# Fourth stage: layer norm moments and roots one step ahead, and its normalising split in pairs between the two exps of two steps

## The reference

```
def _layernorm(x, axis=-1, eps=1e-05):
    m = jnp.mean(x, axis=axis, keepdims=True)
    v = jnp.var(x, axis=axis, keepdims=True)
    return (x - m) / jnp.sqrt(v + eps)
...
    qkv = jnp.einsum('bsd,ed->bse', x, Wqkv)
    ... 16 heads of 8 features
    logits = jnp.einsum('bihd,bjhd->bhij', q, k) * scale + pos_bias[None]
    attn = jax.nn.softmax(logits, axis=-1)
    out = jnp.einsum('bhij,bjhd->bihd', attn, v).reshape(B, S, D)
    return jnp.einsum('bsd,ed->bse', out, Wout)
...
x = x + _L1_attn_ref(_layernorm(x, axis=-1), L1_attn_Wqkv, L1_attn_Wout, L1_attn_Wpos, L1_attn_coeffs)
```

## Time and profile before

| | |
|---|---|
| median of 3 runs | 1625.31 us (1624.47 to 1625.8) |
| profiled execution | 1624.52 us, its span 1622.7 us |
| PE busy | 1510.8 us (93%) |
| DVE busy | 959.7 us (59%) |
| ACT busy | 832.2 us (51%) |
| POOL busy | 588.4 us (36%) |
| granted TensorE clock, mean | 0.977 |
| fourth stage | from the first bias at 824.7 us to the last output projection at 1070.4 us |

### The profile page before, as it was taken

How to read it: one execution, slowest core, us unless ns; L and a number is a source line. 1 busy time by engine, 2 the same in 40 slices (tenths; PEclk the granted TensorE clock), 3 DMA queues, 4 the chain that set the end, 5 groups by cost and what they waited for, 6 DMA issues and landing times.

```text
span 1622.7 us, 39378 instructions
## 1 busy us (share of the span) xinstructions
PE 1510.8 (93%) x15207; PEld 1153.5 (71%) x15207; DVE 959.7 (59%) x2605; ACT 832.2 (51%) x1574; POOL 588.4 (36%) x583
## 2 busy tenths in 40 slices
PE   6999999997999899999988888959999999998998
PEld 5777776665777777777656666647888888885765
DVE  3344443446778756565568878855556766766223
ACT  4554455445777533343456666635556555553431
POOL 4343445424222101111166666632323344434024
PEclk9999999998999999999999999979999999999999
DMA  5021230000000099100000000000000000000323
GB/s 151 16 60 40 61 106 7 12 1 8 8 10 10 2 379 384 65 0 0 1 1 2 2 2 2 2 13 1 6 6 6 12 11 9 7 9 25 97 77 87
DMA packets 76527, 68.85 MB, mean 42 GB/s; under 512 B 19533, under 2 KB 57034, under 8 KB 76234
## 3 DMA queue, kind: packets, MB, share of 16 engines
q1 hardware_dynamic: 74314, 62.36, 11.9%
q0 software_dynamic: 2048, 4.20, 0.8%
HBM read 24.58 MB, written 41.96 MB: 41 GB/s over the span
## 4 chain that ended last, share of the span: by engine, by line
PE 69%; issue 10%; DVE 9%; ACT 6%; POOL 4%; DMA 1%; SPq 1%; POOLq 0%; DVEq 0%; ACTq 0%
PE bank L1874 7%; PE bank L1866 7%; PE bank L2394 5%; PE bank L2362 5%; PE bank L1508 5%; PE bank L2356 4%; PE bank L1492 4%; PE bank L2373 4%; PE bank L2385 3%; PE bank L853 2%; PE bank L3019 2%; PE bank L873 2%; PE bank L826 2%; PE bank L3008 2%; PE bank L3010 2%
## 5 line engine op out<-in xcount | busy, mean ns | idle before, releaser
L1291 ACT COPY s_pT<-bank 77x512 f32<-77x512 f32 (+1 forms) x256 | 134.7, 585 | 91.1 <-PE bank L1492 90.8
L2184 POOL TENSOR_TENSOR s_p<-s_p,s_inverse 128x616 f32<-128x616 f32 x64 | 78.2, 1228 | 229.7 <-DVE s_inverse L2307 229.7
L1492 PE MATMUL bank<-ident,s_p 128*77 128x128 f32 (+1 forms) x1024 | 138.3, 281 | 21.1 <-ACT s_p L1284 20.6
L1726 ACT ACTIVATE s_hT<-bank,w_s_b 128x512 f32<-128x512 f32 x128 | 87.2, 687 | 126.2 <-PE bank L1866 125.1
L1492 PEld LDWEIGHTS bank<-ident,s_p 128*77 128x77 f32 (+1 forms) x1024 | 114.4, 146 | 49.8 <-ACT s_p L1284 31.1
L1874 PEld LDWEIGHTS bank<-w_s_w2T,s_hT 128*128 128x128 f32 x1024 | 122.3, 192 | 26.8 <-issue 15.3
L1195 POOL TENSOR_TENSOR s_p<-s_p,s_peak 128x1024 f32<-128x1024 f32 x64 | 120.0, 1896 | 37.9 <-DVE s_peak L1371 37.9
L1874 PE MATMUL bank<-w_s_w2T,s_hT 128*128 128x128 f32 x1024 | 124.4, 276 | 2.2 <-ACT s_hT L1726 2.2
L1866 PE MATMUL bank<-s_ln_xnT,w_s_w1T 128*128 128x512 f32 x256 | 121.6, 603 | 0.0
L1284 ACT ACTIVATE s_p<-s_p 128x616 f32<-128x616 f32 (+1 forms) x128 | 109.8, 892 | 20.6 <-POOL s_p L1195 16.4
L1827 DVE SCALAR_TENSOR_TENSOR s_total<-bank,s_combine,s_total 128x128 f32<-128x128 f32 x256 | 72.1, 344 | 74.6 <-PE bank L1874 73.2
(11 more groups left out here) (302 smaller groups left out, 3455.0 us busy)
## 6 DMA issues: line engine op xcount, KB each, us to landing
sorted_tokens<-s_zero SPq DMA_DIRECT2D x8, 4096.0 KB, 29.5
s_rows<-sorted_tokens SPq DMA_DIRECT2D x48, 64.0 KB, 1.9
routed_tokens<-s_routed SPq DMA_DIRECT2D x12, 256.0 KB, 2.4
x_all<-x SPq DMA_DIRECT2D x8, 256.0 KB, 3.2
w_s_gateup<-s_gateup SPq DMA_DIRECT2D x1, 2048.0 KB
out<-x_all SPq DMA_DIRECT2D x8, 256.0 KB, 2.7
w_s_k<-ctxT SPq DMA_DIRECT2D x8, 154.0 KB, 2.2
s_ctx<-ctxT SPq DMA_DIRECT2D x8, 154.0 KB, 2.5
```

Of the source, the lines that this page charges most:

```text
L1291: nc.scalar.copy(pT[0:keys, b % 2, 4 * q:4 * q + 4, :].rearrange("m h t -> m (h t)"), bank[0:keys, flip_bank("p", b, q), :]).then_inc(drai ...
L1492: last = nc.tensor.transpose(bank[0:keys, into, j * T:(j + 1) * T], p[:, b % 2, 4 * q + j, :], core.ident[:, :])
L1726: nc.scalar.activation(hT[:, e % 2, c, :], bank[:, HIDDEN + k % 4, :], ACT.Gelu, bias=w.s3_b1[:, k:k + 1]).then_inc(hT_ready, 1)
L2184: nc.gpsimd.tensor_tensor(part, part, inverse[:, b % 2, heads].unsqueeze(2).to_broadcast([P, HU, M]), ALU.mult).then_inc(share_ready, 1)
```

## The change

In the fourth stage alone (the second keeps its order), and for the groups from the second on:

- DVE takes the moments of the next group one step earlier, at the end of step 3 of the group before (`norm_steps` is 0, 3, 7, 11, 15, 19, 23 in place of 0, 4, 8, ...). The first entry stays at step 0, so for the group that is normalised in steps 1 and 2 nothing moves here.
- POOL's four root operations move with them: behind `lower` of the last batch of a group and ahead of `own_of` and `lower` of the next. A wait for `xn_ready` of the group before is added ahead of them, since `rstd` and `shift` have one buffer.
- ACT's four ACTIVATEs at the end of step 1 become two pairs, which stand between exp half 0 and exp half 1: batches 0 and 1 in step 1, batches 2 and 3 in step 2.

The PE program and all shapes and counts of instructions stay.

```diff
+    norm_steps = [G * g if cross or g == 0 else G * g - 1 for g in range(GROUPS - 1)]
...
         def rstd_of(g):
             pool.wait_ge(moments_ready, g + 1)
+            if g and not cross:
+                pool.wait_ge(xn_ready, G * g)
...
-            if g < GROUPS and b % G == 0:
-                rstd_of(g)
+            if b in norm_steps:
+                rstd_of(norm_steps.index(b) + 1)
...
-        def xn_of(g):
+        def xn_of(g, batches=range(G)):
...
-            for n in range(G):
+            for n in batches:
...
             if b >= 0:
                 exp_of(b, 0)
+            if not cross and step % G in (1, 2) and g < GROUPS:
+                xn_of(g, range(step % G * 2 - 2, step % G * 2))
...
-            if step % G == 1 and g < GROUPS:
+            if cross and step % G == 1 and g < GROUPS:
                 xn_of(g)
...
-            if step % G == 0 and g < GROUPS:
-                moments_of(g)
+            if step in norm_steps:
+                moments_of(norm_steps.index(step) + 1)
```

## The result

| | before | after |
|---|---|---|
| median | 1625.24 us (4 runs, 1624.47 to 1625.8) | 1602.14 us (4 runs, 1600.66 to 1602.82) |
| ratio | | 0.9857, 95% interval 0.984 to 0.9874 |
| profiled execution | 1624.52 us, span 1622.7 | 1602.82 us, span 1601.0 |
| granted clock, mean | 0.977 | 0.984 |
| fourth stage, first scores to last output projection | 823.47 to 1070.39: 246.9 us | 823.97 to 1047.07: 223.1 us |

The kernel is 23.1 us faster; 1601.5 was forecast. Two later measurements of the same kernel gave 1601.39 and 1602.24. In the profiled executions the stage alone is 23.8 us shorter, where the sum had 23.7.

A forecast was written before the change was run, and what follows sets the result against it. TensorE was busy 93% of the span; in the fourth stage its waits and a lowered clock bound the norm groups. Six groups at 3.95 us, 23.7, took 1624.52 to 1600.8, plus 0.8: 1601.5 us, range 1598.5 to 1605.

The forecast's parts named there:

- the sum: Fourth stage: 0.89 + 1.56 + 1.67 = 4.1 us a group, taken as 3.95 after the walk; six groups, 23.7 us.
- The moments: Step 1: DVE's bias and `add_to_x` come 1.26 us sooner, so PE's weighing starts 0.89 us sooner.
- the cover: End of step 3: DVE's 1.56 us wait for the scores takes in the moved moments' 1.26 us at no cost.
- The ACTIVATEs: Step 2: the first exp no longer stands behind four normalising ACTIVATEs on ACT; gain 1.56 us a group.
- The clock: Step 2's weighing: without the 1.77 us idle the clock stays up; 1.67 us a group regained, bounds 0 and 1.67.
- What is late next: Step 3: PE's exp hangs on POOL's lowering, behind DVE's bias of step 2; it costs 0.1 us.
- The walk: One group followed link by link through four engines: 26.7 us against 30.68, steps of 6.24, 6.72, 6.22 and 7.55.
- the prediction's 0.1 for them: POOL's moved roots cost between nothing and 1.73 us; 0.1 taken, with keys ready 0.7 us before the scores.
- The second group's norm: Stage's steps 1 and 2: held exp costs at most 1.0 us, at best gives 1.56; taken as 0.
- The signs: Profile after: about 26.7 us a group, no exp wait above 0.5 from the second group, PEclk 1.00 from the first.
- thin covers: Rival: idle times barely hold the moved work; the roots' 1.73 us coming through gives 13.3 us, 1612; chance 0.04.
- fall all the same: Rival: the clock still falls on short idles, leaving 2.3 us a group, 13.7 in all: 1611.6; chance 0.07.

The follow-up runs named there:

- the filler: Kernel before the change, plus 12 throwaway identity transposes on PE ahead of step 2's wait for the exp, in seven groups: 1614.47 us.
- pairs only: Changed kernel with moments and roots back in step 0, the ACTIVATEs still in pairs between the exps: 1607.93 us.
- the first experiment: Changed kernel with the four ACTIVATEs back at the end of step 1, moments and roots still a step early: 1614.46 us.
- the stall: Changed kernel plus four throwaway ACTIVATEs ahead of step 2's first exp in seven groups: 1617.03 us; with 12 throwaway PE transposes as well: 1611.98 us.
- the run that began 1.7 us sooner: Changed kernel with the same order in the second stage too: 1602.57 us, beside 1601.39 for the changed kernel; the execution profiled took 1604.49.

## Why the prediction was right

Point by point, per group:

- *The moments, 0.89 us*: measured alone, 9.09 - 8.20 = 0.89. The wait on which the cover rested shrank to 0.30 us and stayed a wait.
- *The ACTIVATEs, 1.56 us*: with them put back, 1.53; with them alone moved, 1.34, since 0.2 us of the held pair comes through. That the expectation for that kernel had 1.35 is luck: it sets 896.35, at which the prediction lets the transposes start, against 897.70, the start of the exp. ACT's copies ended at 896.14, so without a cost of the held exp the gain would have been 1.56. In the changed kernel the two together take 9.09 - 6.67 = 2.42, and 0.89 + 1.56 = 2.45 was forecast.
- *The clock, 1.67 us*: 7.88 - 6.23 = 1.65, shown alone by the filler; 1.61 in the groups whose step 2 took 7.84.
- *What is late next, -0.1*: the size is right and the place is not. The walk had 7.55 us for step 3, by the bias of step 2; step 3 stayed at 7.51. Step 0 became longer, 6.29 in place of 6.20, where the walk had 6.24, and by the roots: POOL has no idle time around them, and the lowering behind them starts 883.15 - 879.90 = 3.25 us behind step 0's first transposes, where it was 886.67 - 883.51 = 3.16 before. The exp and then PE's transposes of step 1 wait for it. With the roots left in their place (pairs only) step 0 is 6.20 us; so it is with the roots early in the longer groups of the first experiment, where POOL still has 0.52 us of idle time ahead of that lowering. So 0.09 of the roots' 1.73 us comes through; the prediction's 0.1 for them had the spread keys and the scores in mind.
- *The sum, 3.95*: six groups take 1036.73 - 852.88 = 183.85 us before and 1013.40 - 853.29 = 160.11 after: 30.64 - 26.69 = 3.96 a group, 23.7 us in all. (The last addition is off by 0.1: 1600.8 and 0.8 give 1601.6.)
- *The second group's norm, 0*: in the profile after, the third step's first transposes stand 845.79 - 828.62 = 17.17 us behind the second scores, 845.37 - 828.11 = 17.26 before: 0.1 us gained. The 0 was a choice between a cost of 1.0 and a gain of 1.56, not a sum, so that it came out so closely is in part luck. The pair did hold back the exp there, by 2.51 us.
- *The signs*: those named for the stage all stand in the profile after but one. PEclk was to be 1.00 from the first group on; it is 0.50 for some seven microseconds of the first group, as before the change, and 1.00 from the second group on.

Of the rivals, thin covers are refuted for the pair twice: four ACTIVATEs in place of two cost nothing, and a pair held for 2.55 us costs 0.2 us. Of the roots 0.09 us comes through, not 1.73. The clock does not fall all the same: from the second group to the last with a norm the longest idle of PE in the changed kernel is 0.38 us, and no fall follows. That it is the long idle that matters is shown by putting it back: waits of 1.77 us (2.19 in the first group) bring the fall behind four of seven, and the same waits filled behind none. The Trainium skill, "TensorE: Matmul & The Clock Gate", section on a second failure mode (psum-queue depth-cycling), has micro-idles between groups of matmuls make the clock swing between its levels; this trace does not show it: 0.25 to 0.36 us of idle stand ahead of each step's first transposes, and from the second group to the stage's end the clock is 1.00.

What fell short is small and lies outside the stage: the stage gave 23.8 us, the medians of the runs 23.1 and the two profiled executions 21.7. In these the stage begins 0.5 us later after the change, and from the stage's end to the last instruction it is 552.3 us before and 553.9 after in the profiled executions, 552.9 and 553.4 in the two later ones. No run was made to settle where this comes from.

## What to carry to other kernels

Price a move by the distances between starts of one recurring instruction, step by step, and look for a stretch of the same trace that lacks what the move takes away: the last groups without a norm gave 6.68 and 6.19 us for the steps that came out at 6.67 and 6.23. Where a short wait of TensorE stands just ahead of stretched matmuls, the wait costs more than its length (1.56 us of ACT work cost 3.2 with the clock's fall), and filling it with throwaway transposes is a quick test of how much. Before editing away a wait, look for the room that the waiting instruction has: one of 2.55 us in every group cost 0.2 here.

## What the runs showed of the hardware that I had not expected

Waits of PE of one length are not followed by one outcome. The wait of 1.77 us was followed by 1.2 GHz six times out of six in the kernel before, whose groups are 30.6 to 30.7 us long. With only the moments moved it was followed by it every second time, three of six; with the stall put back, too, four of seven. Within each kernel the work around the wait was the same each time. In the kernel before, the 2.15 us wait of the first group was followed by no fall, and in the kernel with the stall one of 2.19 us at the same place was. What decides it was not settled.

A microsecond won at the start of a stretch at the lower clock was lost in it once: in the third stage the run that began 1.7 us sooner (563.52 against 565.24) had the lower mean clock in each of the three windows shown, and was 0.2 us ahead at their end. Each of the two was profiled once.
